# A perceiver block on one core: halves of a rounded operand in one product, output sums from rounded halves, and a weight offset made in an earlier stage

## What is computed

```
x = x + xattn(layernorm(x), ctx)     # softmax(q k^T / 16) v over 4096 context tokens, then (h + attended) Wo^T + bo
x = x + attn(layernorm(x))           # 16 heads of 16, causal, three heads with a region weight
x = x + ffn(layernorm(x))            # soft mixture: 64 experts x 32 slots

logits  = (h @ phi_w^T + phi_b).reshape(t, z, 64, 32)
D, C    = softmax(logits, axis=3), softmax(logits, axis=2)
X_tilde = tanh(normalise(clip(einsum('tznp,tzd->npd', D, h))))
Y_tilde = einsum('npd,ndH->npH', X_tilde, expert_w) + expert_b
Y       = einsum('tznp,npH->tzH', C, Y_tilde)
```

## Time and profile before

| | us |
|---|---|
| median of 3 runs (all: 577.39, 581.51, 581.21) | 581.21 |
| the profiled execution | 578.23 |
| its span | 576.4 |
| TensorE busy | 541.2 (94%) |
| VectorE busy | 345.5 (60%) |
| ScalarE busy | 357.7 (62%) |
| GpSimd busy | 350.6 (61%) |

### The profile page before, as it was taken

The page is one execution under the profiler, slowest core; times in us unless marked ns, Lnnn a source line. Parts: engine busy times, 40 slices in busy tenths (PEclk is TensorE's granted clock), DMA queues, the critical chain, the costliest instruction groups (busy, mean ns, idle before and its releaser), DMA issues. The chain is left out here.

```text
span 576.4 us, 9531 instructions
## 1 busy us (share of the span) xinstructions
PE 541.2 (94%) x3384; PEld 429.5 (75%) x3384; DVE 345.5 (60%) x695; ACT 357.7 (62%) x1000; POOL 350.6 (61%) x271
## 2 busy tenths in 40 slices
PE   5998999999999999998997977879999999999998
PEld 4786998999899999887666655445555886777786
DVE  1784444464456445536787896787999999334100
ACT  2437665766576857853887973339999885554300
POOL 2775986667666764644579697244576889906000
PEclk9999999999999999999899998999999999999999
DMA  8454445454434333176069400400000907877100
GB/s 290 155 220 147 147 146 182 149 202 146 162 131 146 146 117 103 48 148 136 2 169 213 168 2 0 148 1 1 0 1 1 195 24 232 280 218 221 38 19 18
DMA packets 37056, 70.22 MB, mean 122 GB/s; under 512 B 3217, under 2 KB 27153, under 8 KB 35985
## 3 DMA queue, kind: packets, MB, share of 16 engines
q1 hardware_dynamic: 37010, 69.62, 39.3%
HBM read 65.42 MB, written 4.19 MB: 121 GB/s over the span
## 5 line engine op out<-in xcount | busy, mean ns | idle before, releaser
L380 POOL TENSOR_TENSOR ctxT_lo<-front,ctxT_hi 128x1024 fp32r<-128x1024 f32 x32 | 76.8, 2405 | 55.3 <-ACT ctxT_hi L661 55.3
L385 POOL TENSOR_TENSOR ctx_lo<-ctx_in,ctx_hi 128x1024 fp32r<-128x1024 f32 x32 | 76.7, 2400 | 17.2 <-ACT ctx_hi L666 17.2
L494 PE MATMUL ps<-ctx_hi,pT_hi 128*128 128x256 f32 x256 | 75.4, 295 | 1.8 <-DVE pT_lo L832 1.8
L496 PE MATMUL ps<-ctx_hi,pT_lo 128*128 128x256 f32 x256 | 72.4, 283 | 0.0
L495 PE MATMUL ps<-ctx_lo,pT_hi 128*128 128x256 f32 x256 | 72.3, 283 | 0.0
L685 ACT CAST pT_hi<-ps 128x512 fp32r<-128x512 f32 x64 | 34.0, 591 | 42.1 <-PE ps L476 42.1
L1740 PE MATMUL ps<-front,turned 128*128 128x512 f32 x128 | 59.7, 593 | 0.3 <-PEq L978 0.3
L1788 PE MATMUL ps<-front,comb 128*128 128x256 f32 x256 | 57.8, 381 | 0.0
L824 DVE TENSOR_SCALAR_CACHE_REDUCE first<-ps,qbk 128x512 f32<-128x512 f32 x32 | 24.0, 750 | 55.5 <-PE ps L464 53.1
L1788 PEld LDWEIGHTS ps<-front,comb 128*128 128x128 f32 x256 | 47.6, 190 | 7.6 <-issue 1.6
L832 DVE TENSOR_TENSOR pT_lo<-ps,pT_hi 128x512 fp32r<-128x512 f32 x64 | 41.1, 686 | 17.4 <-ACT pT_hi L685 17.4
(11 more groups left out here) (235 smaller groups left out, 1345.2 us busy)
## 6 DMA issues: line engine op xcount, KB each, us to landing
front<-in_ctx_turned_dram SPq DMA_DIRECT2D x32, 512.0 KB, 4.3
ctx_in<-in_ctx_dram SPq DMA_DIRECT2D x32, 512.0 KB, 3.3
back<-in_L_ffn_expert_w_dram SPq DMA_DIRECT2D x11, 1024.0 KB, 5.5
turned<-in_L_ffn_expert_w_dram SPq DMA_DIRECT2D x5, 1024.0 KB, 7.7
front<-in_phi_turned_dram SPq DMA_DIRECT2D x1, 2048.0 KB
front<-in_L_ffn_expert_b_dram SPq DMA_DIRECT2D x4, 512.0 KB, 10.3
qk_parts_dram<-first SPq DMA_DIRECT2D x4, 384.0 KB, 5.1
qk_parts_dram<-qk_parts SPq DMA_DIRECT2D x4, 384.0 KB, 2.9
```

The costliest lines, as they stand in the source:

```text
L380: nc.gpsimd.tensor_tensor(ctxT_lo[:, n % RING, :, :], turned_in[:, n % SLOTS, :, :], ctxT_hi[:, n % RING, :, :].bitcast(F32), ALU.subtract ...
L385: nc.gpsimd.tensor_tensor(ctx_lo[:, m % RING, :], ctx_in_sb[:, m % SLOTS, :], ctx_hi[:, m % RING, :].bitcast(F32), ALU.subtract).then_inc( ...
L494: nc.tensor.matmul(pO[q][:, 0:D], pT_hi[:, c % 2, q, cols], hi, start=c == 0 and j == 0, stop=False)
L496: last = nc.tensor.matmul(pO[q][:, 0:D], pT_lo[:, c % 2, q, cols], hi, start=False, stop=c == NCH - 1 and j == J - 1)
```

## The change

1. In cross attention both halves of the context stand in one tensor `ctx_both`, by tile first hi then lo, and one product of 512 columns makes hi x hi and hi x lo into two halves of a PSUM bank. VectorE scales the first half and adds the scaled second one in another pass.
2. phi less its first row is made in cross attention in four pieces of 1024 columns: SP loads a piece and the first row's part, GpSimd subtracts, SP stores it to `phi_dram`, in chunks 14 to 29 of the loads. Self attention only loads the result. The row of ones of the first half comes with VectorE's copy (two scalars per partition) instead of by a memset.
3. The output sum of the mixture takes three fp32r products instead of one in fp32. ScalarE's copy of a turned block rounds it (`comb_hi`), VectorE subtracts (`combine_low`); for the experts' outputs ScalarE copies (`outputs_high`), VectorE subtracts (`outputs_low`). A bank of a turned block is free after VectorE's subtraction. In steps 4 to 7 the last two blocks are turned after the experts' product. VectorE's sums of tiles 4 to 7 stand in steps 8 to 11. After step 15 turned blocks are spread between the output sums. Some statistics share one semaphore.

```diff
-                        nc.tensor.matmul(pO[q][:, 0:D], pT_hi[:, c % 2, q, cols], hi, start=c == 0 and j == 0, stop=False)
-                        nc.tensor.matmul(pO[q][:, 0:D], pT_hi[:, c % 2, q, cols], lo, start=False, stop=False)
-                        last = nc.tensor.matmul(pO[q][:, 0:D], pT_lo[:, c % 2, q, cols], hi, start=False,
-                                                stop=c == NCH - 1 and j == J - 1)
+                        nc.tensor.matmul(pO[q][:], pT_hi[:, c % 2, q, cols], ctx_both[:, m % RING, j, :, :].rearrange("p k d -> p (k d)"),
+                                         start=c == 0 and j == 0, stop=c == NCH - 1 and j == J - 1, skip_group_check=True)
+                        last = nc.tensor.matmul(pO[q][:, 0:D], pT_lo[:, c % 2, q, cols], ctx_both[:, m % RING, j, 0, :], start=False,
+                                                stop=c == NCH - 1 and j == J - 1, skip_group_check=True)
...
-                    nc.vector.tensor_scalar(att[:, q, :], pO[q][:, 0:D], rinv[:, q:q + 1], None, ALU.mult).then_inc(att_v, 1)
+                    nc.vector.tensor_scalar(att[:, q, :], pO[q][:, 0:D], rinv[:, q:q + 1], None, ALU.mult).then_inc(half_v, 1)
+                for q in range(QT):
+                    dve.wait_ge(half_v, QT * b + q + 1)
+                    nc.vector.scalar_tensor_tensor(out=att[:, q, :], in0=pO[q][:, D:2 * D], scalar=rinv[:, q:q + 1], in1=att[:, q, :],
+                                                   op0=ALU.mult, op1=ALU.add).then_inc(att_v, 1)
...
+            def load_phi(k):
+                at_least(sp, phi_out, 16 * k)
+                cols = slice(k % 2 * PIECE, (k % 2 + 1) * PIECE)
+                sp.dma_start(phi_piece[:, 0, :], phi_turned[:, k * PIECE:(k + 1) * PIECE]).then_inc(phi_in, 16)
+                sp.dma_start(phi_piece[:, 1, :], phi_turned[0:1, cols].broadcast_to([P, PIECE])).then_inc(phi_in, 16)
+
+            def store_phi(k):
+                first = 1 if k < 2 else 0
+                sp.wait_ge(phi_g, k + 1)
+                sp.dma_start(phi_dram[first:, k * PIECE:(k + 1) * PIECE], phi_piece[first:, 0, :]).then_inc(phi_out, 16)
...
-            sp.dma_start(kept.front[:], phi_turned).then_inc(phi_in, 16)
-            sp.dma_start(phi_row, phi_turned[0:1, 0:SL].broadcast_to([P, SL])).then_inc(phi_in, 16)
-            sp.wait_ge(phi_g, SL // 512)
-            sp.dma_start(kept.front[0:1, 0:SL], phi_b.rearrange("(o s) -> o s", o=1)).then_inc(phi_in, 16)
-            sp.wait_ge(phi_in, 48)
+            sp.dma_start(kept.front[:], phi_dram).then_inc(phi_in, 16)
+            sp.wait_ge(phi_in, 16)
...
-                if i >= GROUPS // 2:
-                    less_first_column(i - GROUPS // 2)
...
-                    nc.vector.tensor_copy(hT[:, 0, HALF:2 * HALF], PS_TURN[0][:]).then_inc(pro_v, 1)
+                    dve.wait_ge(pro_v, 1)
+                    nc.vector.tensor_scalar(hT[:, 0, HALF:2 * HALF], PS_TURN[0][:], rest_rows[:], ident[:, 0:1],
+                                            ALU.mult, ALU.add).then_inc(pro_v, 1)
...
-                    at_least(pe, cT_a, LB * c + k - 1)
+                    at_least(pe, cTlo_v, LB * c + k - 1)
...
-                    pe.wait_ge(mixed_v, s + 1)
-                    last = nc.tensor.matmul(psY[t], comb[:, t, s * P:(s + 1) * P], mixed[:, s, :],
-                                            start=s == 0 and (t >= TT // 2 or t % 2 == 0), stop=s == ST - 1,
+                    pe.wait_ge(ylo_v, s + 1)
+                    cols = slice(s * P, (s + 1) * P)
+                    nc.tensor.matmul(psY[t], comb_hi[t][:, cols], y_hi[:, s, :], start=s == 0 and (t >= TT // 2 or t % 2 == 0),
+                                     stop=False, skip_group_check=True)
+                    nc.tensor.matmul(psY[t], comb_hi[t][:, cols], y_lo[:, s, :], start=False, stop=False, skip_group_check=True)
+                    last = nc.tensor.matmul(psY[t], comb_lo[:, t, cols], y_hi[:, s, :], start=False, stop=s == ST - 1,
                                             skip_group_check=True)
...
+            def outputs_high(s):
+                act.wait_ge(mixed_v, s + 1)
+                nc.scalar.copy(y_hi[:, s, :], mixed[:, s, :]).then_inc(yhi_a, 1)
...
+            def combine_low(c, first, end):
+                for k in range(first, end):
+                    cols = slice(k * 512, (k + 1) * 512)
+                    dve.wait_ge(cT_a, LB * c + k + 1)
+                    nc.vector.tensor_tensor(comb_lo[:, c, cols], psC[k % 2][:], comb_hi[c][:, cols].bitcast(F32),
+                                            ALU.subtract).then_inc(cTlo_v, 1)
+
+            def outputs_low(s):
+                dve.wait_ge(yhi_a, s + 1)
+                nc.vector.tensor_tensor(y_lo[:, s, :], mixed[:, s, :], y_hi[:, s, :].bitcast(F32), ALU.subtract).then_inc(ylo_v, 1)
...
-                outputs(s)
-                if s < 2:
-                    input_statistics(s + 6)
-                if s in (2, 4, 9, 11):
-                    combine_invert(SLOTWISE + (2, 4, 9, 11).index(s))
+                turn = turned_at(s)
+                if turn is not None:
+                    combine_low(turn[0], turn[1], turn[1] + 2)
+                if s:
+                    outputs(s - 1)
+                if 1 <= s <= 2:
+                    input_statistics(s + 5)
+                if turn is not None:
+                    combine_low(turn[0], turn[1] + 2, turn[2])
+                if s >= 2:
+                    outputs_low(s - 2)
+                if 8 <= s < 12:
+                    combine_invert(SLOTWISE + s - 8)
```

More of the change, by code:

```diff
@@ L350, in _ @@
                 load_turned(n)
+                k, step = divmod(n - PIECE_AT, PIECE_EVERY)
+                if 0 <= k < 4 and step == 0:
+                    load_phi(k)
+                if 0 <= k < 4 and step == 3:
+                    store_phi(k)
                 if n == 2 * NCH:
@@ L412, in _ @@
                     second_scale(b - 2)
+                k, step = divmod(n + 2 - PIECE_AT, PIECE_EVERY)
+                if 0 <= k < 4 and step == 0:
+                    pool.wait_ge(phi_in, 32 * (k + 1))
+                    nc.gpsimd.tensor_tensor(phi_piece[:, 0, :], phi_piece[:, 0, :], phi_piece[:, 1, :], ALU.subtract).then_inc(phi_g, 1)
             def projection_bias(first, end):
@@ L1412, in last_attended @@
                 for q in range(QT):
-                    nc.vector.tensor_scalar(kept.att[:, q, :], bank[6 + q][:, 0:D], kept.rinv[:, q:q + 1], None, ALU.mult).then_inc(att_v, 1)
+                    nc.vector.tensor_scalar(kept.att[:, q, :], bank[6 + q][:, 0:D], kept.rinv[:, q:q + 1], None, ALU.mult).then_inc(half_v, 1)
+                for q in range(QT):
+                    dve.wait_ge(half_v, q + 1)
+                    nc.vector.scalar_tensor_tensor(out=kept.att[:, q, :], in0=bank[6 + q][:, D:2 * D], scalar=kept.rinv[:, q:q + 1],
+                                                   in1=kept.att[:, q, :], op0=ALU.mult, op1=ALU.add).then_inc(att_v, 1)
             def last_sums():
@@ L1533, in sem @@
             return st.enter_context(nc.semaphore(name))
+        with nc.sbuf_tensor("comb_lo", [P, TT, SL], F32R) as comb_lo:
+            pass
         comb = sb("comb", [P, TT, SL])
+        with nc.sbuf_tensor("xc_hi", [P, SL], F32R) as xc_hi:
+            pass
         xc = sb("xc", [P, 2 * KEPT_PAIRS, D])
@@ L1656, in _ @@
         def _(pool):
[L1657 to L1658 removed]
+            nc.gpsimd.memset(power[:], -0.5).then_inc(rstd_g, 1)
+            pool.wait_ge(rstd_g, 1)
             pool.wait_ge(xve_v, 1)
@@ L1838, in _ @@
                         pe.wait_ge(clip_v, 14 if t < 2 else ST)
-                        pe.wait_ge(cT_a, LB * (t + 1))
+                        pe.wait_ge(cTlo_v, LB * (t + 1))
                     if end > first:
                         mix(t, first, end)
+                    if t == 0 and turn is not None and turn[2] > turn[1] + 2:
+                        transpose_combine(turn[0], turn[1] + 2, turn[2])
             experts(ST - 1)
-            transpose_combine(TT - 2, 0, LB)
             for t in range(TT // 2):
-                last = mix(t, mixed_until(t, ST - 1), ST)
+                if t < 2:
+                    transpose_combine(TT - 2, t, t + 1)
+                mix(t, mixed_until(t, ST - 1), ST - 1)
+            for t in range(TT // 2):
+                last = mix(t, ST - 1, ST)
                 if t % 2:
                     last.then_inc(y_mm, 2)
-            transpose_combine(TT - 1, 0, LB)
-            for t in range(TT // 2, TT):
-                pe.wait_ge(cT_a, LB * (t + 1))
+                    transpose_combine(TT - 2, t // 2 + 2, t // 2 + 3)
+            pe.wait_ge(cTlo_v, LB * (TT // 2 + 1))
+            for k in range(LB):
+                transpose_combine(TT - 1, k, k + 1)
+                last = mix(TT // 2, k * LB, (k + 1) * LB)
+            last.then_inc(y_mm, 1)
+            for t in range(TT // 2 + 1, TT):
+                pe.wait_ge(cTlo_v, LB * (t + 1))
```

(2 more changed lines are left out.)

121 lines of the change are left out of this document (71 added, 50 removed).

## The result

The changed kernel took 606.86 us (median of 4 runs, 605.18 to 609.99) where the kernel before took 580.19 on the same chip: ratio 1.047, 95% interval 1.041 to 1.054. The forecast was 572.0 with a range of 563 to 583. The profiled execution took 609.99 us, span 608.2, against 578.23 and 576.4 before.

A forecast was written before the change was run, and what follows sets the result against it. TensorE, 94% busy, was taken to bound the kernel, notably in cross attention and the output sums. Terms -2.8-5.2-0.6-5.8+0.6+4.7+1.5 = -7.6 us, put on the mean of 579.6, gave 572.0 us, range 563 to 583.

The forecast's parts named there:

- The step that failed: Cross attention: SP's wait for GpSimd's phi subtraction ahead of the next chunk's loads is hidden, 1 us if not.
- Cross attention pair, -2.8: Cross attention: three 256-column products (0.360 us) become one of 512 and one of 256 (0.349), 256 times: -2.8 us.
- Self attention, -5.2: Self attention: without GpSimd's subtractions, groups after group 9 take 4.5 us each: -5.2 us, bounds -1.5 and -7.
- Row of ones, -0.6: Ahead of the mixture: making the row with VectorE's copy removes a GpSimd step on the path: -0.6 us.
- After step 15, -5.8: Mixture's end: output sums of three 0.120 us products instead of 0.432 us shorten 38.6 us to 32.8: -5.8 us.
- Steps 4 to 7, +0.6: Expert steps: less TensorE work, but waits for turned blocks' banks, 21.1 us to 21.8: +0.6 us, bounds -2.9 and +3.
- Steps 8 to 15, +4.7: Expert steps: VectorE's four back-to-back sums and low halves held by GpSimd make TensorE wait: +4.7 us, +1.9 without those holds.
- Rival 1: Expert steps: low halves wait until GpSimd has nothing more queued, so the kernel is slower, 588 us; chance 0.12.
- Clock behind step 13, +1.5: Expert steps: half clock follows the last wait of step 13: +1.5 us, bounds 0 and +4.
- Rivals 2 and 3: 2: low halves pass freely, clock stays, self attention faster, 566 us, chance 0.16; 3: self attention gains only 1.5, 578, 0.14.

The follow-up runs named there:

- experiment 1: Changed kernel with the first two phi stores taking all 128 partitions instead of 127: 575.71 us, ratio 0.9935.
- experiment 2: Changed kernel with rows 1 to 127 of phi stored as two transfers of 112 and 15 partitions: 575.49 us, ratio 0.9937.
- experiment 4: Kernel before with only the phi pieces made in cross attention, stores of 128 partitions: 576.51 us, ratio 0.9949.
- experiment 5: Kernel before with the mixture's part alone (rounded halves, sums in steps 8 to 11, row of ones by VectorE): 581.13 us, ratio 1.0024.
- 6b: Experiment 1's kernel, sums in steps 8, 10, 12 and behind step 15, first three low halves behind the first turned block: 573.64 us, ratio 0.9905.
- 6c: 6b with the reciprocal that releases GpSimd's divisions behind the next step's output sum and low half: 571.65 us, ratio 0.985.
- 7b: 6c with sums in steps 7, 9, 11, 13, each reciprocal a step later, and the row of ones by memset: 567.98 us, ratio 0.978.

## Why the prediction was wrong

**The step that failed** is "SP waits for it ahead of the next chunk's loads, about one chunk late out of four loaded ahead: hidden, and 1 us if not". "It" was GpSimd's subtraction. The stage has a second wait, `load_phi`'s for the landing of the store before it, and a store with a shape of its own, 127 partitions; I looked at the stage's DMA share and at neither. Experiments 1, 2 and 4 put that step's cost at 30.8 us with 127 partitions and 0.0 with 128. I bounded it by 0 and 1 us, although no row of before showed a store of 127 partitions, so that nothing measured stood behind either bound. Beside this the Trainium skill (DMA: Bandwidth & Descriptors, Why a DMA increments its semaphore by 16 and not by 1) has the rule by which 127 partitions go through one engine; it names that very number, and the prediction did not weigh it.

**The other terms**, each from the table (experiment 1 against before):

- *Cross attention pair, -2.8.* Measured -1.1. The second pair of a chunk and the last, six pairs on, in two chunks:

```profile
64.20 0.40 PE L521 MATMUL ps<-ctx_both,pT_hi 128*128 128x512 f32 x1
...
66.29 0.39 PE L521 MATMUL ps<-ctx_both,pT_hi 128*128 128x512 f32 x1
...
77.10 0.40 PE L521 MATMUL ps<-ctx_both,pT_hi 128*128 128x512 f32 x1
...
79.22 0.40 PE L521 MATMUL ps<-ctx_both,pT_hi 128*128 128x512 f32 x1
```

  64.20 to 66.29 us is 0.348 a pair, as forecast, but two chunks on, 77.10 to 79.22, it is 0.353. There the mix of a chunk takes 2.91 us instead of 2.96, and the scores behind it 2.78 instead of 2.75: chunks are 6.48 us apart and not 6.41. What makes products of 512 columns a little slower there stays open.
- *Self attention, -5.2.* Measured -5.7. From group 10 on the sum was right, 26.67 us to the last transposes where I had 27.0 and before had 32.27, and no VectorE operation of over 2 us is left. The single groups were not the even 4.5 us that I had: 5.6, 3.8, 5.2, 4.2, 5.2 and 2.7. These 26.7 us stand in all ten profiles with phi made earlier. The groups ahead of them do not: in five of the ten, experiment 4 among them, the half clock came behind waits of under 2 us at group 7 (eight products of L1251 in 3.2 to 3.7 us instead of 1.99), and the stage took 92.4 to 93.6 us instead of 90.8 to 91.0. That the forecast fitted so closely here is in part luck.

```profile
358.12 0.60 PE L1227 MATMUL ps<-ident,eB 128*128 128x128 f32 x4
...
384.79 0.60 PE L1227 MATMUL ps<-ident,eB 128*128 128x128 f32 x4
```

- *Row of ones, -0.6.* The wait is 2.56 us instead of 3.02, -0.5; in experiment 5 the stage took 112.70 instead of 113.25. In the changed kernel and in experiment 1 the half clock came behind it, +1.7, which I had not forecast.
- *After step 15, -5.8.* Measured -6.1.
- *Steps 4 to 7, +0.6, bounds -2.9 and +3.* Experts 0 to 7 measured +2.5: mis-sized within its bounds. The waits were not what was wrong in the sum: 2.60 us for the first turned block's subtraction, where I had 1.8, behind low halves that were held too (1.56 us), and 0.84 later where I had 1.8, 3.4 in all for 3.6. TensorE's own work from the first transposes of step 4 to those of step 8 was longer, 20.1 us for my 18.2, and by the same products at full clock some 1.7 of that is the half clock behind the first wait, which I had looked for behind step 13 only (granted clock 0.54 over 519.0 to 521.1 us; the second eight transposes take 1.99 us instead of 1.04):

```profile
517.07 1.68 PE L1792 MATMUL ps<-ident,comb 128*128 128x128 f32 x8 [2.60 <-DVE comb_lo L2080]
518.55 0.63 PE L1800 MATMUL ps<-ident,xh 128*128 128x128 f32 x2
519.22 1.99 PE L1792 MATMUL ps<-ident,comb 128*128 128x128 f32 x8
...
530.57 1.04 PE L1792 MATMUL ps<-ident,comb 128*128 128x128 f32 x8
```

  It came so in all six profiles with this order of VectorE, and in none of 6b, 6c and 7b, where the waits there are 0.7 us each.
- *Steps 8 to 15, +4.7.* Measured +4.5, experts 7 to 15 from 31.0 to 35.5 us. The chain is the predicted one. A low half takes 1.43 us beside GpSimd where I had 1.3, a sum 3.85 for 3.80, and VectorE is free at 559.5, 23.6 us after 535.9, where I had 24.0:

```profile
549.56 3.89 DVE L2030 TENSOR_REDUCE csum<-comb 128x32 f32<-128x2048 f32 x1
549.70 0.38 PE L1818 MATMUL ps<-y_hi,first_hi 128*128 128x256 f32 x1 [1.87 <-DVE y_lo L2085]
...
553.92 5.18 POOL L1711 TENSOR_TENSOR comb<-comb,cinv 128x512 f32<-128x512 f32 x4 [0.63 <-DVE cinv L2032]
554.04 1.43 DVE L2085 TENSOR_TENSOR y_lo<-front,y_hi 128x256 fp32r<-128x256 f32 x1
555.39 3.78 DVE L2030 TENSOR_REDUCE csum<-comb 128x32 f32<-128x2048 f32 x1
...
560.25 1.22 PE L1792 MATMUL ps<-ident,comb 128*128 128x128 f32 x8 [2.81 <-DVE comb_lo L2080]
561.40 1.53 PE L1810 MATMUL ps<-back,xhT 128*32 128x256 f32 x16
```

  The rule quoted from the Trainium skill (SBUF — State Buffer, Who interferes with whom) held for the form that no row of before had. Rival 1 fell: no low half lost a second end.
- *Clock behind step 13, +1.5.* There in the changed kernel's profile (experts in 1.53 us instead of 1.09, the next ones 5.26 us on instead of 3.81) and not in experiment 1's; among the six profiles with this order it came in two.

Rivals 2 and 3 fell as well: no low half beside GpSimd passed freely, and in self attention no hold took the place of the 5.08 us one.

Without the failed step the forecast stood 3 us off: -7.6, against -4.6 between the profiles of experiment 1 and before once the start is left out (575.8-576.4 = -0.6, less 57.18-53.19 = 4.0), and against -4.3 by medians (575.71 and 580.01). The 3 us are the pair (1.7) and steps 4 to 7 (1.9), less 0.6 that the other terms gave more. In that 0.6 two misses of the clock nearly cancel, which is luck: +1.7 behind the row of ones, where none was forecast, and -1.5 behind step 13, where it was.

## What to carry to other kernels

Before costing a new transfer at nothing, write down its number of partitions, who waits for its landing and what is queued behind: 127 instead of 128 partitions made each of two 0.5 MB stores some 20 us long and cost 31 us together, and a buffer that spares the wait brought back only 3. When work is moved to a less busy engine, spread it so that no step holds more of it than the neighbour's step is long; here the experts' steps took 8 us less with the same four sums in steps 7, 9, 11 and 13 instead of 8 to 11 and the low halves moved out of the way, 1.5 us of it because the half clock behind the shortened wait stayed away. And put an operation that another engine's work holds up (0.40 us alone, 1.41 beside it) ahead of the one that releases that work.

## What was not expected of the hardware

- A slow store of 127 partitions also lengthens the issue of other transfers on its queue: 6.92 us for a load that takes 0.33 otherwise, as shown above, with and without SP's wait.
- The start has two lengths. In the profiles of the twelve kernels the first mix stands at 52.9 to 53.9 us in seven and at 57.2 to 57.4 in five, and where it is late TensorE's first products ran at half the clock, 3.60 us (experiment 1) against 1.97 (experiment 2) for the same eight:

```profile
15.71 3.60 PE L474 MATMUL ps<-h1T,phib 128*128 128x256 f32 x8 [0.34 <-DVE small L947]
```
```profile
13.27 1.97 PE L474 MATMUL ps<-h1T,phib 128*128 128x256 f32 x8 [0.34 <-DVE small L947]
```

  That is 4 us of difference between two kernels whose code is the same up to there, more than most terms of this study; 4.1 of the 31.8 us between the spans of before and changed are of this kind. A ledger by stages, from the first mix on, is free of this one, but each later half clock moves its stage by some 1.5 to 1.7 us in the same way.
- The same wait (2.56 us, at the row of ones) was followed by the half clock in the changed kernel and by the full one in experiment 5. The form of the row does not decide it; whether the phi part moved ahead does, or chance, one trace of each kernel cannot tell.
